# The projection of an attention and mixture-of-experts block: rotary products straight from PSUM, the first normalisation on ScalarE, and stores by half sequences

## The reference: what is computed

```python
x = L0_attn_x                                   # (8, 1024, 256)
y = _layernorm(x, axis=-1)                      # (y - mean) / sqrt(var + 1e-5)
q, kv = y @ Wq, y @ Wkv                         # each 256 wide: 16 heads of 16
q, kv = split(q), split(kv)                     # (8 * 16, 1024, 16)
q, kv = _apply_rotary(freqs, q), _apply_rotary(freqs, kv)
#   t * cos + concat([-x2, x1]) * sin, x1 and x2 the two halves of a head's 16
att = softmax(q @ kv.T / 4); out = att @ kv     # kv is key and value
x = x + out @ Wout + bout
x = x + experts(_layernorm(x))                  # 8 experts of 1024 tokens each
```

## Time and profile before

| | us |
|---|---|
| median of three runs (lowest, highest) | 2242.66 (2234.14, 2255.21) |
| the profiled execution, its own time | 2249.14 |
| its span | 2247.3 |
| TensorE, VectorE, ScalarE, GpSimd busy in the span | 2015.3, 1947.7, 1503.4, 649.2 |
| stores `qkv_parts`, number and size | 64 of 512 KB |
| stores `values`, loads `p_x` | 8 of 1024 KB, 16 of 512 KB |

### The profile page before, as it was taken

One profiled execution on the slowest core, in us unless ns is written; L12 is line 12 of the kernel. 1 busy time (PEld: TensorE's weight loads), 2 busy tenths in 40 slices (PEclk: granted clock), 3 DMA queues, 4 the chain that ended last, 5 costly groups with the idle time before them and its releaser, 6 DMA issues. The chain is left out here.

```text
span 2247.3 us, 53242 instructions
## 1 busy us (share of the span) xinstructions
PE 2015.3 (90%) x16684; PEld 1046.1 (47%) x16684; DVE 1947.7 (87%) x3221; ACT 1503.4 (67%) x2842; POOL 649.2 (29%) x864
## 2 busy tenths in 40 slices
PE   6777699999999999999999999999898129999998
PEld 3333233333333333333333333333476118999997
DVE  7887879999999999999999999999299668888863
ACT  3444268888888888888888888888545004554443
POOL 7788201110110111011101110111277014555653
PEclk9999679999999999999999999999999559999999
DMA  2666632444344444433443444343486023433432
GB/s 89 219 224 204 182 92 69 83 82 77 71 83 83 74 74 81 85 73 75 82 85 70 78 81 80 72 80 71 145 273 202 23 85 74 105 87 90 98 68 29
DMA packets 152687, 224.69 MB, mean 100 GB/s; under 512 B 34871, under 2 KB 105114, under 8 KB 152602
## 3 DMA queue, kind: packets, MB, share of 16 engines
q1 hardware_dynamic: 131958, 197.96, 36.7%
q0 software_dynamic: 12288, 17.05, 4.5%
q10 hardware_dynamic: 8356, 8.67, 1.1%
HBM read 129.45 MB, written 93.06 MB: 99 GB/s over the span
## 5 line engine op out<-in xcount | busy, mean ns | idle before, releaser
L761 DVE TENSOR_REDUCE a_mx<-a_sm 128x2 f32<-128x1024 f32 x1024 | 1235.5, 1223 | 69.6 <-PE a_sm L709 54.0
L836 ACT ACTIVATE a_prob<-a_st 128x512 f32<-128x512 f32 x2048 | 1113.2, 597 | 180.5 <-PE a_st L672 150.0
L709 PE MATMUL a_sm<-a_k,a_q 48*128 48x512 f32 x2048 | 759.1, 460 | 9.3 <-DVE a_mx L761 7.6
L672 PE MATMUL a_st<-a_q,a_k 50*128 50x512 f32 x2048 | 761.3, 452 | 5.8 <-DMA a_q<-a_mrow 5.8
L696 PE MATMUL a_pv<-a_prob,a_v 128*32 128x256 f32 x8192 | 660.7, 394 | 22.9 <-ACT a_oraw L843 22.3
L672 PEld LDWEIGHTS a_st<-a_q,a_k 50*128 50x128 f32 x2048 | 313.0, 187 | 415.0 <-ACT a_prob L836 395.5
L696 PEld LDWEIGHTS a_pv<-a_prob,a_v 128*32 128x32 f32 x8192 | 162.2, 108 | 404.7 <-issue 198.1
L811 POOL TENSOR_TENSOR a_v<-a_v_raw,a_zero 128x256 f32<-128x256 f32 x64 | 39.6, 620 | 1052.5 <-DMA a_v_raw<-values 1002.9
L709 PEld LDWEIGHTS a_sm<-a_k,a_q 48*128 48x128 f32 x2048 | 306.2, 189 | 21.2 <-DVE a_mx L761 19.2
L1751 ACT ACTIVATE e_hT<-e_ps_h,e_b1b 128x512 f32<-128x512 f32 x128 | 88.3, 690 | 207.5 <-PE e_ps_h L1788 203.8
L1788 PE MATMUL e_ps_o<-e_w_high,e_hT_high 128*128 128x256 f32 x512 | 145.9, 285 | 0.0
(11 more groups left out here) (146 smaller groups left out, 2362.5 us busy)
## 6 DMA issues: line engine op xcount, KB each, us to landing
qkv_parts<-p_parts SPq DMA_DIRECT2D x64, 512.0 KB
a_q<-qkv_parts SPq DMA_DIRECT2D x128, 128.0 KB, 3.5
a_k<-qkv_parts SPq DMA_DIRECT2D x128, 128.0 KB, 4.3
attended<-a_oraw SPq DMA_DIRECT2D x64, 256.0 KB, 3.9
e_w<-in_fc_dram SPq DMA_DIRECT2D x16, 1024.0 KB, 5.2
token_table<-f_tab ACTq DMA_DIRECT2D x8, 1056.0 KB, 4.9
p_x<-in_x_dram SPq DMA_DIRECT2D x16, 512.0 KB, 8.5
values<-p_values SPq DMA_DIRECT2D x8, 1024.0 KB, 20.2
```

Source lines behind the costliest of these rows:

```text
L672: nc.tensor.matmul(st[:, slot % RING], kb[rows, q.buf, jt * P:(jt + 1) * P], qb[rows, q.buf, ic * CHUNK:(ic + 1) * CHUNK], start=True, sto ...
L709: mm = nc.tensor.matmul(sm[:, slot, h], qb[rows, q.buf, qt * P:(qt + 1) * P], kb[rows, q.buf, kc * CHUNK:(kc + 1) * CHUNK], start=True, st ...
L761: nc.vector.tensor_reduce(mx[:, qt, kc, :], sm[:, slot], AX.X, ALU.max, negate=True).then_inc(max_done, 1)
L836: nc.scalar.activation(prob[:, jt % 2, h, ic * CHUNK:(ic + 1) * CHUNK], st[:, slot % RING], ACT.Exp, scale=DH ** -0.5).then_inc(drained, 1)
```

## The change

The rotary products are both made by VectorE from PSUM; there is no `qkv`, no `projected`, no `cos_product` and no `first_sum`. `ps_q` has four buffers instead of two. The columns of the weights are reordered on the host so that the first halves of all heads (for q and k) come first, then the second halves, and the signs in `rot_sin` are turned. GpSimd makes the sum, all 512 columns in two instructions of 256, and writes them back to the order of heads. ScalarE normalises: `x * rstd + shift` with `shift = -mean * rstd`, which VectorE makes for four tiles at once. The lags grow: the last is 13 instead of 11. Stores of parts go out for four tiles (a half sequence) in eight transfers of 256 KB, 2 KB for each partition, and one load of x stands between two such stores; `values` still goes out once for a sequence. The SyncE loop is unrolled. `load_first` comes after the first two of the last four half-sequence stores of parts.

```diff
-    NORM, PROJ, TURN, SUM, BACK, CUT = 6, 7, 8, 9, 10, 11
-    FIRST = P
+    SHIFT, NORM, TURN, TURNED, PROJ, ROTATE, SUM, BACK, HIGH, CUT = 2, 6, 6, 7, 8, 9, 10, 11, 12, 13
+    QBANKS = 4
...
-    ps_q = mem.ps("p_ps_q", [P, 2, 4 * P])
+    ps_q = mem.ps("p_ps_q", [P, QBANKS, 2 * D])
...
+        def store(it, h):
+
+            done = it * STEP + (h + 1) * GROUP
+            s, cols = h // 2, slice(h % 2 * GROUP * P, (h % 2 + 1) * GROUP * P)
             sp.wait_ge(high_done, done)
             sp.wait_ge(low_done, done)
             for c in range(4):
                 kind, chunk = c // 2, c % 2
                 for part in range(CUTS):
...
+                    first = (it * SEQS + s) * H + chunk * 8
+                    sp.dma_start(parts_dram[first:first + 8, kind, part, :, cols],
+                                 parts[:, s, c, part, cols].bitcast(F32)).then_inc(parts_out[h], 16)
+            if h % 2 == 1:
+                sp.wait_ge(values_done, done)
+                sp.dma_start(v_dram[it * SEQS + s].rearrange("r p n -> p r n"),
+                             values[:, s].rearrange("p r i h e -> p r (i h e)")).then_inc(v_out[s], 16)
...
+        for it in range(PASSES):
+            for h in range(GROUPS):
+                if it > 0:
+                    store(it - 1, h)
+                if h < 2 and it > 0:
+                    load(it, h + 2)
+                elif h >= 2 and it + 1 < PASSES:
+                    load(it + 1, h - 2)
+        for h in range(GROUPS):
+            if h == 2:
+
+                for first in range(2):
+                    sp.wait_ge(parts_out[first], 16 * 4 * CUTS)
+                sp.wait_ge(v_out[0], 16)
+                load_first(sp)
+            store(PASSES - 1, h)
...
-        def normalise(it, k, n):
-            dve.wait_ge(rstd_done, it * GROUPS + (k // GROUP + 1))
+        def shift_of(it, k, n):
+            g = k // GROUP
+            cols = slice(g * GROUP, (g + 1) * GROUP)
+            dve.wait_ge(rstd_done, it * GROUPS + (g + 1))
+            nc.vector.scalar_tensor_tensor(out=shift[:, cols], in0=mv[:, cols, 0], scalar=-1.0, in1=rstd[:, cols],
+                                           op0=ALU.mult, op1=ALU.mult).then_inc(shift_done, 1)
+
+        def rotate(it, k, n):
+
+            i = k % TILES
+            dve.wait_ge(q_done, n + 1)
             if past(n, 2):
...
+                dve.wait_ge(rot_done, 2 * (n - 1))
+            nc.vector.tensor_tensor(t_cos[:, k % 2].rearrange("p (x d) -> p x d", d=HALF),
+                                    ps_q[:, k % QBANKS].rearrange("p (x d) -> p x d", d=HALF),
+                                    cosb[:, i:i + 1, 0:HALF].to_broadcast([P, 4 * H, HALF]),
                                     ALU.mult).then_inc(cos_done, 1)
...
+            nc.vector.tensor_tensor(t_sin[:, k % 2].rearrange("p (o x d) -> p o x d", o=2, d=HALF),
+                                    ps_q[:, k % QBANKS].rearrange("p (o x d) -> p o x d", o=2, d=HALF),
+                                    sinb[:, i].rearrange("p (o d) -> p o d", o=2).unsqueeze(2)
+                                    .to_broadcast([P, 2, 2 * H, HALF]), ALU.mult).then_inc(sin_done, 1)
...
+        def add(it, k, n):
             pool.wait_ge(cos_done, n + 1)
-            pool.wait_ge(sin_done, n * 2 + 2)
+            pool.wait_ge(sin_done, n + 1)
             if past(n, 2):
...
                 pool.wait_ge(rT_done, n - 1)
                 pool.wait_ge(values_done, n - 1)
-            nc.gpsimd.tensor_tensor(rot[:, k % 2, FIRST:], t_cos[:, k % 2, FIRST:], t_sin[:, k % 2, FIRST:], ALU.add
-                                    ).then_inc(rot_done, 1)
+            for h in range(2):
+                to = rot[:, k % 2].rearrange("p (x h d) -> p x h d", h=2, d=HALF)[:, :, h]
+                own, other = (buf[:, k % 2, of * D:(of + 1) * D].rearrange("p (x d) -> p x d", d=HALF)
+                              for buf, of in ((t_cos, h), (t_sin, 1 - h)))
+                nc.gpsimd.tensor_tensor(to, own, other, ALU.add).then_inc(rot_done, 1)
...
+        def normalise(it, k, n):
+            act.wait_ge(shift_done, it * GROUPS + (k // GROUP + 1))
+            if past(n, 2):
+
+                act.wait_ge(xT_done, n - 1)
+            nc.scalar.activation(xn[:, k % 2], xb[:, k], ACT.Identity, bias=shift[:, k:k + 1],
+                                 scale=rstd[:, k:k + 1]).then_inc(xn_done, 1)
...
         def high_part(it, k, n):
             s, i = k // TILES, k % TILES
+            if k % GROUP == 0 and past(it):
+
+                act.wait_ge(parts_out[k // GROUP], 16 * 4 * CUTS * it)
             if i == 0 and past(it):
...
                 act.wait_ge(v_out[s], 16 * it)
...
-            for stage, lag in ((turned_tokens, NORM), (projected, PROJ), (high_part, BACK)):
+            for stage, lag in ((normalise, NORM), (turned_tokens, TURNED), (high_part, HIGH)):
...
-            for stage, lag in ((turn_tokens, NORM), (products, PROJ), (turn_back, BACK)):
+            for stage, lag in ((turn_tokens, TURN), (products, PROJ), (turn_back, BACK)):
```

More of the change, by code:

```diff
@@ L120, in project @@
     rstd = mem.sb("p_rstd", [P, STEP])
+    shift = mem.sb("p_shift", [P, STEP])
     mhalf = mem.sb("p_mhalf", [P, GROUP])
@@ L137, in project @@
     x_in = [a.sem(f"p_x_in{g}") for g in range(GROUPS)]
-    parts_out = [a.sem(f"p_parts_out{s}") for s in range(SEQS)]
+    parts_out = [a.sem(f"p_parts_out{h}") for h in range(GROUPS)]
     v_out = [a.sem(f"p_v_out{s}") for s in range(SEQS)]
@@ L148, in project @@
     q_done = a.sem("p_q_done")
-    qkv_done = a.sem("p_qkv_done")
+    shift_done = a.sem("p_shift_done")
     cos_done = a.sem("p_cos_done")
@@ L201, in sync, with stored @@
             load(0, g)
[L202 to L209, removed]
+        for it in range(PASSES):
+            for h in range(GROUPS):
+                if it > 0:
+                    store(it - 1, h)
[10 more added lines that the diff above has]
+            store(PASSES - 1, h)
+    def stored(sp):
+        for h in range(GROUPS):
+            sp.wait_ge(parts_out[h], 16 * 4 * CUTS * PASSES)
         for s in range(SEQS):
[L211 to L216, removed]
             sp.wait_ge(v_out[s], 16 * PASSES)
@@ L275, in body @@
         def body(it, j):
-            for stage, lag in ((statistics, 0), (normalise, NORM), (cos_product, TURN), (low_part, CUT),
-                               (first_sum, SUM)):
+            tile = flow.at(it, j, 0)
+            if tile:
+                statistics(*tile)
+            tile = flow.at(it, j, SHIFT)
+            if tile and tile[1] % GROUP == GROUP - 1:
+                shift_of(*tile)
+            for stage, lag in ((rotate, ROTATE), (low_part, CUT)):
                 tile = flow.at(it, j, lag)
@@ L323, in body @@
                 inverse_root(*tile)
-            tile = flow.at(it, j, TURN)
+            tile = flow.at(it, j, SUM)
             if tile:
-                turn(*tile)
-        pool.wait_ge(consts_in, 64)
+                add(*tile)
         pool.wait_ge(halves_set, 2)
-        flow.run(pool, body, TURN)
+        flow.run(pool, body, SUM)
     def scalar(act):
+        def normalise(it, k, n):
[4 more added lines that the diff above has]
+                                 scale=rstd[:, k:k + 1]).then_inc(xn_done, 1)
         def turned_tokens(it, k, n):
@@ L363, in body @@
                     stage(*tile)
-        flow.run(act, body, BACK)
+        flow.run(act, body, HIGH)
     def tensor(pe):
```

82 lines of the change are left out of this document (15 added, 67 removed).

## The result

The changed kernel took 2230.98 us in the median of 11 runs (2221.76 to 2237.12), the kernel before 2245.98 (11 runs, 2234.14 to 2255.21): a ratio of 0.993, interval 0.9912 to 0.9949. That is 15 us gained, 0.7%. The forecast was 2238, within 1%, gaining 4.5 us. The direction held; the gain was three times the forecast. The profiled execution took 2231.27 us with a span of 2229.4, against 2249.14 and 2247.3.

A forecast was written before the change was run, and what follows sets the result against it. It took the transfers, with stores on 8 of 16 engines, to bound the projection, VectorE close behind. Starting stores sooner gains 4.5 us: 2249.1 - 4.5 = 2244.6 profiled, less 6.5 for the runs' median, 2238 us; range 2214 to 2262.

The forecast's parts named there:

- the bound: Projection: transfers set its pace at 28.2 us per sequence, stores filling 8 of 16 engines; VectorE close behind at 25.8.
- the first maxima: End of projection: TensorE starts attention's maxima at 233 to 246 us, about 239, against 243.5; 4.5 us gained.
- start of the first store: SyncE's queue: the first store of parts goes out after four tiles, at about 38 us, not at 50.2.
- the 2 KB penalty: Stores of parts: 2 KB packets are 8% dearer than 4 KB, so a half-sequence store takes 10.9 us.
- the loss: SyncE held at loads behind full queues: 7% over the pure transfer sum before, about half of it expected after.
- After that point nothing changes.: Attention after its first loads: maxima 32.9 us, then the first pair 35.3 us at 1.2 GHz, both as before.
- the clock: Attention's first pair: 35.3 us at half clock again; staying at 2.4 GHz was part of a rival with chance 0.14.
- no loop of waits is longer than it: Projection: no loop of waits exceeds TensorE's 2.44 us per tile; the longest found was about 3.6 us for two tiles.
- Sixteen engines: Rival: the new store destination spreads over 16 engines, start of maxima at about 195, 2195 us; chance 0.06.
- SyncE as the bound: Rival: each store issue costs SyncE 1.5 us, 16.2 us a quarter, maxima 20 us late, 2262 us; chance 0.14.
- Products held up at 1.14 us: Rival: VectorE's products from PSUM take 1.14 us each, 3.4 us per tile, 2243 us; chance 0.06.
- The better transfers: Rival: no 2 KB penalty and no loss, or the clock stays at 2.4 GHz; about 2222 us, chance 0.14.

The follow-up runs named there:

- The pair on sixteen engines: Changed kernel and kernel before, each with qkv_parts reordered so that a store's destination is 128 rows, not 8 heads: 2185.9 and 2219.5 us.
- second trace: Each kernel traced once more, unchanged: changed kernel 2228.3 us, kernel before 2243.0 us, one execution each.
- the two part kernels: Changed kernel with the old SyncE program, 2270.2 us; kernel before with the new SyncE program, 2237.1 us.
- With the low part first: Changed kernel with the old SyncE program, VectorE making the low part ahead of the statistics in each step: 2231.9 us, ratio 0.9942 to the kernel before.
- the engines' part alone: Changed kernel with the old SyncE program (512 KB stores of whole sequences): 2270.2 us, ratio 1.0123 to the kernel before.

## Why the prediction was right, and where it was off

**Right: the bound.** The share of 0.51 read as half of the engines full, and 26.4 to 28.2 us per sequence of transfers beside 25.8 of VectorE, was the right picture. Taking some 6 us per sequence from VectorE and 10 from GpSimd moved the pace by nothing (28.2) or 1.7 us (26.5). The pair on sixteen engines shows what they were worth without that bound.

**Right, with errors that cancel: the first maxima.** Forecast 239, measured 238.4 and 231.7. By the terms, for the first trace:
- start of the first store 35.6, not 38: -2.4.
- the 2 KB penalty. The forecast took 8% from a pair of rows with different traffic; the stores ran at 204 GB/s against 209, so a half-sequence store is 2.10 MB / 204 = 10.3 us, not 10.9: 14 x 0.6 = -8.4. This is the most mis-sized term, and its lower bound (none) was closer. By the share (0.53 for 204 GB/s) the penalty comes out at 6%, so how much of this and of the next term is penalty and how much is loss stays open; their sum is what is measured.
- the loss. The pure sum is now 35.6 + 14 x 10.3 + 22.4 + 16 = 218.2. The last `values` ahead of the loads was issued at 222.3 and landed 9.9 us later, at 232.2: 14 us lost, 7%, the same share as before. I had taken half of it, 6.5, because single loads should block SyncE less: +7.4. In the second trace, whose first store starts at 37.4, it landed at 215.3 + 11.6 = 226.9: 7 us lost, half. The assumption was a guess, and it holds in one trace of two.
- from there to the maxima 6.2 us, not 4: +2.2.

**Wrong: "After that point nothing changes."** This sentence stood on the stretch rows alone. The 32.9 us from maxima to scores had 5.8 us of waiting for a small DMA in them, which one look at the waits of that stretch would have shown; the edit makes the stores before it smaller and fewer. Cost: 5.6 us of the gain missed (5.2 in the second traces). That it comes from the SyncE program is shown by the two part kernels, 5.0 us of waiting with the old one and 27.9 us from maxima to scores with the new one; size and number of the stores aren't separated.

**Wrong, or not forecast: the clock.** The prediction expected 35.3 us at half clock again and gave its return only as part of a rival. The first pair of scores came 5.7 us cheaper (2.9 in the second traces). That this is the change's doing isn't shown: the time from the first scores to the return was 35.3 and 24.5 us in two traces of the same kernel before, and 9.0 to 37.9 over the other ten, with no order by store size or engines that I could find. What orders it stays open. So do 5.4 us that the second pair of traces gives back after the second pair of heads, and the 1.5 us more that the first gains there.

**Incomplete: "no loop of waits is longer than it".** Two were missed: store, load, statistics, low part, store, which the large stores close and the half-sequence stores only shorten (30.8 us of waiting for `x` in the change, 64.6 with large stores); and TensorE's turn-back behind the low part. The stores by half sequences, costed as a mere earlier start, are what makes the engines' part pay in the order of operations that the change has: without them it loses 1.2%. With the low part first it pays without them (0.9942).

**The rivals.** Sixteen engines didn't come by themselves; made so, the price of 2195 was 9 us too high. SyncE as the bound at 1.5 us for an issue is refuted by 0.56 us on sixteen engines. Products held up at 1.14 us: refuted by 0.681 and 0.686. The better transfers (no penalty) hold in the penalty, not in the loss. The table of the Trainium skill, "DMA: Bandwidth & Descriptors", section "Bandwidth", measured on loads that GpSimd issues, has 32% of peak at 64 KB and 78% at 1 MB, so by it 256 KB would be at about half of peak, an estimate. The traces don't bear that out where several stores stand in the queue: 204 GB/s at 256 KB against 209 at 512 KB on eight engines, and 340 GB/s at 256 KB on sixteen.

## What to carry to other kernels

A DMA share that stands at one half with work in the queue is a bound, and engines made faster behind it buy little: 15 us here, and 33.6 with the bound gone. Look at the outermost dimension of the destination first, which here, with the changed kernel otherwise the same, took off a further 1.9% (0.993 to 0.9746). Where one engine feeds a store and also waits for a load, put the operation that frees the store ahead of the one that waits: a lag that is two steps longer can close a loop through a transfer queue. And before writing "nothing changes from here", list that stretch's waits for small DMAs, since they stand behind whatever stores the edit has resized or moved.

## What the runs showed of the hardware

- SyncE's time at an issue followed how full the DMA engines were. Eight stores of 512 KB: about 12 us on eight engines (kernel before), 7.9 to 8.9 on sixteen. Eight of 256 KB: 6.8 to 12.1 in the kernel after and 4.5 to 5.5 on sixteen. A load of 512 KB behind a store and `values`: 4.6 to 6.3 us in the kernel after, at most 0.9 on sixteen; behind a large store and `values` 12.2 us with the engines' part alone and 1.5 on sixteen.
- The loads of q and k, in packets of 4 KB to few partitions (at most 32 packets a transfer), filled the engines at a low rate: in the 6.4 us before the first maxima of the kernel after, the share was 1.05 at 142 GB/s. That is 0.4 to 0.5 us for a packet, an estimate from share and rate that takes all packets as 4 KB.

```profile
232.00:238.40 6.40, 0.00 (x0) 0.02 (x1) 0.00 (x0) 0.00 (x0) 0.00 (x0) 0.50 1.05 142
```

- VectorE with one operand in PSUM kept 0.68 us for 128x512 beside a GpSimd that took 0.73 us a sum; with both in SBUF it had a median of 1.14.
- With TensorE busy without a gap, the return of the granted clock from 0.50 to 1.00 took 9 to 38 us in twelve traces of this stage.
